# A selective scan on one core: GpSimd multiplies four state tiles by C in one instruction, and VectorE ends the softplus

## The reference

```python
xp = x @ W_xproj
dt, Bm, Cm = jnp.split(xp, [DT_RANK, DT_RANK + D_STATE], axis=-1)
dt = jax.nn.softplus(dt @ W_dt + b_dt)
A = -jnp.exp(A_log)
...
dA = jnp.exp(dt_t[:, :, None] * A)
dBu = (dt_t * u_t)[:, :, None] * B_t[:, None, :]
h = dA * h + dBu
y = jnp.einsum('bdn,bn->bd', h, C_t)
```

## Time and profile before

| | |
|---|---|
| median of 3 runs | 8623.25 us |
| the profiled execution: span | 8660.7 us |
| mean granted TensorE clock, as a share of 2.4 GHz | 0.819 |
| busy over the span: PE, DVE, ACT, POOL | 73%, 77%, 51%, 64% |
| first to last product by C (the middle stage) | 2617.2 to 8146.1 us |

### The profile page before, as it was taken

One profiled execution on the slowest core, in us unless ns is written; L12 is line 12 of the kernel. 1 busy time (PEld: TensorE's weight loads), 2 busy tenths in 40 slices (PEclk: granted clock), 3 DMA queues, 4 the chain that ended last, 5 costly groups with the idle time before them and its releaser, 6 DMA issues. The chain is left out here.

```text
span 8660.7 us, 103591 instructions
## 1 busy us (share of the span) xinstructions
PE 6299.7 (73%) x30668; PEld 2526.0 (29%) x30668; DVE 6682.6 (77%) x7810; ACT 4408.3 (51%) x5988; POOL 5534.1 (64%) x2731
## 2 busy tenths in 40 slices
PE   6888888888876667767767777767776666766455
PEld 3444444444431222222222222222222222222133
DVE  3555555555548999999999999999999999999634
ACT  1222222222226666666666666666666676766400
POOL 0000000000009999999999999999999999999600
PEclk8898888898887888888888888887888888778666
DMA  1111111111115556555555555555655555555553
GB/s 30 43 45 39 43 45 37 45 44 38 45 35 192 196 190 206 184 199 199 186 205 190 191 207 184 200 196 187 209 185 199 200 185 206 190 194 202 140 152 128
DMA packets 513971, 1253.45 MB, mean 145 GB/s; under 512 B 170085, under 2 KB 172297, under 8 KB 513673
## 3 DMA queue, kind: packets, MB, share of 16 engines
q1 hardware_dynamic: 513417, 1252.41, 43.5%
q0 software_dynamic: 512, 0.53, 0.0%
HBM read 943.30 MB, written 231.21 MB: 136 GB/s over the span
## 5 line engine op out<-in xcount | busy, mean ns | idle before, releaser
L1180 DVE TENSOR_TENSOR_SCAN b_h<-b_a,b_h 128x448 f32<-128x448 f32 x3584 | 3675.1, 1073 | 273.4 <-POOL b_h L1005 133.9
L1017 POOL TENSOR_TENSOR b_h<-b_h,b_ct 128x896 f32<-128x896 f32 x1792 | 3688.7, 2086 | 28.2 <-DVE b_h L1180 20.0
L1108 ACT ACTIVATE b_a<-b_dts,decay 128x441 f32<-128x441 f32 x3584 | 2228.2, 629 | 1579.4 <-DVE b_h L1180 1558.5
L1267 PE MATMUL b_b<-b_rows,spread_b 16*128 16x512 f32 (+1 forms) x1792 | 690.1, 778 | 1503.1 <-DVE b_h L1170 1502.1
L1028 POOL MEMSET b_seq<- 128x938 f32 x2 | 1.7, 880 | 2499.4 <-POOLq L792 2499.4
L1170 DVE TENSOR_TENSOR b_h<-b_dus,b_b 128x896 f32<-128x896 f32 x1344 | 1432.2, 1066 | 83.1 <-DMA b_dus<-d_dtu 77.7
L1275 PE MATMUL b_y<-b_h,fold 128*32 128x512 f32 (+1 forms) x7168 | 942.5, 652 | 7.8 <-POOL b_h L1017 7.8
L1005 POOL TENSOR_TENSOR b_h<-b_dus,b_bt 128x896 f32<-128x896 f32 x448 | 934.7, 2086 | 10.7 <-DMA b_dus<-d_dtu 10.7
L490 DVE TENSOR_TENSOR a_xg<-a_xd,a_pb 128x784 f32<-128x784 f32 x512 | 495.1, 967 | 512.0 <-PE a_pb L604 510.0
L1267 PEld LDWEIGHTS b_b<-b_rows,spread_b 16*128 16x128 f32 x1792 | 166.0, 226 | 1771.4 <-DVE b_h L1170 1769.8
L1236 PE MATMUL b_w<-b_seq,w_conv 128*128 128x384 f32 (+1 forms) x896 | 553.4, 781 | 12.6 <-DMA b_seq<-b_seq 12.6
(11 more groups left out here) (210 smaller groups left out, 8773.9 us busy)
## 6 DMA issues: line engine op xcount, KB each, us to landing
b_bt<-d_rows SPq DMA_DIRECT2D x448, 448.0 KB, 6.1
b_ct<-d_rows SPq DMA_DIRECT2D x448, 448.0 KB, 3.9
b_dts<-d_dt SPq DMA_DIRECT2D x448, 448.0 KB, 6.0
b_dus<-d_dtu SPq DMA_DIRECT2D x448, 448.0 KB, 6.1
a_xd<-a_xn SPq DMA_DIRECT2D x256, 196.0 KB, 3.4
d_dt<-b_dt SPq DMA_DIRECT2D x112, 448.0 KB, 2.6
d_dtu<-b_soft SPq DMA_DIRECT2D x112, 448.0 KB, 2.5
b_seq<-b_seq SPq DMA_DIRECT2D x112, 234.0 KB, 3.5
```

Source lines behind the costliest of these rows:

```text
L1017: nc.gpsimd.tensor_tensor(hh[t][:], hh[t][:], ct[t // 4 % 2][:], ALU.mult).then_inc(hc_done, 1)
L1108: a(steps(bank(aa, k)), steps(half(dts[t % 4], k)), ACT.Exp, scale=decay[:, t % 4, t // 4:t // 4 + 1]).then_inc(a_done, 1)
L1180: v.tensor_tensor_scan(half(hh[t], k), bank(aa, k), half(hh[t], k), 0.0, ALU.mult, ALU.add).then_inc(h_done, 1)
L1267: last = mm(bb[:, lo:hi], spread_b[q, row, :], rows[i][q, lo:hi], start=True, stop=True)
```

## The change

The 16 tiles `h[t]` become slices of one tile `h_all`. GpSimd multiplies a whole row (128 x 3584) in one instruction at t == 3, 7, 11, 15, C being read four times over. Softplus is written as max(v, ln(1 + exp(min(v, 20)))): with CAP = 20, ScalarE takes relu(CAP - v) out of PSUM, then Exp of CAP minus that, then Ln; VectorE takes the maximum of that and v, straight from PSUM (`step`), at t == 7. GpSimd keeps the product with u alone, behind t == 7. ScalarE's last four moves out of `b_w` come one tile later.

```diff
-                hh = ring("h", HH)
+                h_all = sb("h", [P, HH, TB])
+                hh = [h_all[:, t, :] for t in range(HH)]
...
                         def store_dt(par, o):
-                            sp.wait_ge(dt_ready, o)
+                            sp.wait_ge(moved, o)
...
-                        def products(j, o):
-                            pool.wait_ge(l_ready, o)
-                            nc.gpsimd.tensor_tensor(dtb[:], dtb[:], soft[:], ALU.add).then_inc(dt_ready, 1)
-                            pool.wait_ge(dt_ready, o)
+                        def step_input(j, c):
+                            pool.wait_ge(moved, c + 2)
                             nc.gpsimd.tensor_tensor(soft[:], dtb[:], u[j][:], ALU.mult).then_inc(dtu_ready, 1)
...
-                                pool.wait_ge(h_done, half_no(i, t, 1, it))
-                                nc.gpsimd.tensor_tensor(hh[t][:], hh[t][:], ct[t // 4 % 2][:], ALU.mult).then_inc(hc_done, 1)
-                                if t == 6 and more:
-                                    products(1 - i, unit_no(i, it) + 1)
+                                if t % 4 == 3:
+                                    pool.wait_ge(h_done, half_no(i, t, 1, it))
+                                    row = h_all[:, t - 3:t + 1, :]
+                                    nc.gpsimd.tensor_tensor(row, row, ct[t // 4 % 2][:].unsqueeze(1).broadcast_to([P, 4, TB]),
+                                                            ALU.mult).then_inc(hc_done, 4)
+                                if t == 7 and more:
+                                    step_input(1 - i, spot(i, "pre", it, kind))
...
                                 if t == 10 and i == 0 and kind != LAST:
-                                    sequences(spot(0, "z", it, kind), it + 1, tile_no(0, 10, it))
+                                    sequences(spot(0, "z", it, kind), it + 1, tile_no(0, 7, it))
...
                         def softplus_start(c):
                             act.wait_ge(made, c + 2)
-                            a(soft[:], ww[:, 0:TB], ACT.Abs, bias=dt_bias[:]).then_inc(abs_ready, 1)
-                            a(dtb[:], ww[:, 0:TB], ACT.Relu, bias=dt_bias[:]).then_inc(moved, 1)
+                            a(soft[:], ww[:, 0:TB], ACT.Relu, bias=dt_cap[:], scale=-1.0).then_inc(cap_ready, 1)
                         def softplus_end(o):
-                            act.wait_ge(abs_ready, o)
-                            a(soft[:], soft[:], ACT.Exp, scale=-1.0).then_inc(e_ready, 1)
+                            act.wait_ge(cap_ready, o)
+                            a(soft[:], soft[:], ACT.Exp, bias=cap_col[:], scale=-1.0).then_inc(e_ready, 1)
...
-                                if t == 8 and more:
+                                if t == 9 and more:
...
-                                if t == 10 and more:
+                                if t == 11 and more:
...
-                                if t == 12 and finals:
+                                if t == 13 and finals:
...
-                                if t == 14 and finals:
+                                if t == 15 and finals:
...
+                        def step(c, o):
+                            dve.wait_ge(l_ready, o)
+                            dve.wait_ge(made, c + 2)
+                            v.scalar_tensor_tensor(dtb[:], ww[:, 0:TB], dt_bias[:, 0:1], soft[:], ALU.add, ALU.max).then_inc(moved, 1)
...
+                                if t == 7 and not (kind == LAST and i == 1):
+                                    dve.wait_ge(dt_stored[i], 16 * it + 16 * i)
+                                    step(spot(i, "pre", it, kind), unit_no(i, it) + 1)
```

More of the change, by code:

```diff
@@ L44 @@
 RC = 8
+CAP = 20.0
 SMALL = 21
@@ L115, in program @@
         dt_bias = sbuf("dt_bias", [P, 1])
+        dt_cap = sbuf("dt_cap", [P, 1])
+        cap_col = sbuf("cap_col", [P, 1])
         decay = sbuf("decay", [P, 4, 4])
@@ L258, in _ @@
                     v.memset(one_col[:], 1.0).then_inc(zeroed, 1)
-                    dve.wait_ge(zeroed, 10)
+                    v.memset(cap_col[:], CAP).then_inc(zeroed, 1)
+                    dve.wait_ge(zeroed, 11)
                     dve.wait_ge(masks, 17)
@@ L291, in _ @@
                     link(v.tensor_copy(w_dt_full[:], pd[:, 0:DI]))
+                    link(v.tensor_scalar(dt_cap[:], dt_bias[:], -1.0, CAP, ALU.mult, ALU.add))
                     link(v.tensor_scalar(decay[:], decay[:], -1.0, -1e-12, ALU.mult, ALU.min))
@@ L785, in phase_b @@
                 sq_ready, rstd_ready, xn_ready, seq_ready = (sem(n) for n in ("sq", "rstd", "xn", "seq"))
-                abs_ready, e_ready, l_ready, dt_ready, dtu_ready = (sem(n) for n in ("abs", "e", "l", "dt", "dtu"))
+                cap_ready, e_ready, l_ready, dtu_ready = (sem(n) for n in ("cap", "e", "l", "dtu"))
                 skip_ready, yz_ready, gate_ready = (sem(n) for n in ("skip", "yz", "gate"))
@@ L900, in unit @@
                             if more:
-                                store_dt(par, o)
+                                store_dt(par, spot(i, "pre", it, kind) + 2)
                                 sp.wait_ge(moved, spot(i, "xp", it, kind) + 2)
@@ L939, in _ @@
                         shift_seq(1)
-                        store_dt(0, 2)
+                        store_dt(0, START.index("pre") + 2)
                         sp.wait_ge(moved, START.index("xp") + 2)
@@ L1004, in inputs @@
                             pool.wait_ge(folded, row_no(i, m, it) - 4)
-                            nc.gpsimd.tensor_tensor(hh[4 * m][:], dus[0][:], bt[m % 2][:], ALU.mult).then_inc(pb_done, 1)
+                            nc.gpsimd.tensor_tensor(hh[4 * m], dus[0][:], bt[m % 2][:], ALU.mult).then_inc(pb_done, 1)
                         def unit(i, it, kind):
@@ L1031, in _ @@
                         sequences(None, 1, None)
-                        products(0, 2)
+                        step_input(0, START.index("pre"))
                         inputs(0, 0, 1)
@@ L1120, in unit @@
                                 if t == 5 and more:
-                                    act.wait_ge(dt_stored[i], 16 * it + 16 * i)
                                     act.wait_ge(dtu_stored[i], 16 * it + 16 * i)
@@ L1169, in inputs @@
                                 dve.wait_ge(folded, row_no(i, t // 4, it) - 4)
-                            v.tensor_tensor(hh[t][:], dus[t % 4][:], bb[:, 0:TB], ALU.mult).then_inc(b_done, 1)
+                            v.tensor_tensor(hh[t], dus[t % 4][:], bb[:, 0:TB], ALU.mult).then_inc(b_done, 1)
                         def scan(t, i, it):
@@ L1213, in unit @@
                                     residual(spot(0, "out", it, kind), it - 1)
+                                if t == 7 and not (kind == LAST and i == 1):
+                                    dve.wait_ge(dt_stored[i], 16 * it + 16 * i)
+                                    step(spot(i, "pre", it, kind), unit_no(i, it) + 1)
                         v.memset(aa[:], 0.0).then_inc(aa_zero, 1)
+                        step(START.index("pre"), 2)
                         turns(unit)(dve)
```

## The result

The changed kernel takes 8847.76 us (median of 4 runs, 8829.70 to 8861.43) against 8624.98 us before: ratio 1.025, 95% interval 1.0228 to 1.0272. One of the four executions of the kernel before took 12958.84 us, and the ratio leaves it out. The changed kernel is slower by 2.5%, beyond the range on record (8495 to 8735). The profiled execution spans 8827.9 us.

What follows compares the result with a forecast made beforehand. GpSimd was taken as full and binding, 98.8 us a turn; the new circle summed 8.1 + 2.1 + 2.7 + 10.4 + 26.1 = 49.4 us a unit, 98.8 a turn, so no change: 8622 us, range 8495 to 8735.

Steps and rivals of the forecast that it cites:

- the circle: Row 1 on GpSimd, product with u, store, six loads, input 1, scan of tile 7: 49.4 us a unit.
- VectorE's floor: VectorE's own turn, with no wait for GpSimd or DMA: 96.1 us.
- GpSimd's saving: On GpSimd, row product 8.05 us and softplus add gone: turn 93.2 us, 5.6 less than now.
- VectorE's instruction: New VectorE instruction per unit at tile 7: 1.0 us, less 0.9 us of ScalarE wait, net 0.12 us a unit.
- The circle, first terms: From the end of the scan of tile 7: row 1 8.1 us, product with u 2.1, store and release 2.7.
- Six loads, 10.4 us: SyncE's loads dus 0 to dus 1 on the circle: 10.4 us, from 11.1 before less 0.7 for ct 3.
- The share of 1.00: DMA engines' share where these six loads run; taken to speak for the upper end between about 7.5 and 11.1 us.
- I cancel the two: Earlier sequences frees SyncE for dts 2 to dus 3, perhaps 0.3 us a unit; offset by queueing behind later loads.
- Rival 2: SyncE's queue between store of dt x u and dus 1: loads later still, 8701 to 8745 us; chance 0.13.
- Tied circles: Forecast case: both circles tied within 0.9 us a turn, no change, 8622 us, own range 8565 to 8680; chance 0.50.
- Rivals 3 and 4: TensorE's conv at the low clock each time, 8770, chance 0.05; GpSimd's row not cheaper, 8655 to 8728, chance 0.07.
- Rival 1: VectorE's own work sets the pace, dus 1 earlier or row shorter: 8473 us, partly reached 8475 to 8560; chance 0.25.

Runs made afterwards that it cites:

- row product alone, SyncE's order: Kernel before with the row product, SyncE storing dt x u ahead of rows and loading dus 0, bt 0, bt 1 ahead of ct 3: 8657.55 us, ratio 1.0022.
- dt x u first, SyncE's order: Changed kernel, product with u ahead of row 1, its store ahead of rows, dus 0, bt 0, bt 1 ahead of ct 3: 8566.2 us, ratio 0.9904.
- softplus part alone: Changed kernel with the product per tile put back and sequences waiting for tile 10 as before: 8552.63 us, ratio 0.9913.
- softplus part alone, SyncE's order: Changed kernel, product per tile, store of dt x u ahead of rows, dus 0, bt 0, bt 1 ahead of ct 3: 8606.62 us, ratio 0.9952.
- dt x u first: Changed kernel with one statement moved, the product with u ahead of row 1's product on GpSimd: 8622.63 us, ratio 0.9988.
- row product alone: Kernel before with GpSimd's row product, softplus as before, sequences waiting for tile 7: 8858.3 us, ratio 1.0246.
- changed, dus 1 ahead: Changed kernel with the load of dus 1 moved from sixth to second on SyncE's queue: 8809.12 us, ratio 1.0196.
- tiles, dt x u late: Changed kernel with product per tile, product with u behind tile 10's product, ct 3 loaded ahead of the store of dt x u: 9204.11 us, ratio 1.0652.

## Why the prediction was wrong

Two things are set side by side for every kernel. The first is how far behind the end of the scan of tile 7 dus 0 is issued, as a mean over the 92 to 103 units of each trace whose scan ends between 3000 and 8000 us. The second is VectorE's wait for dus in the stretch from 4400 to 5400.

| kernel | dus 0 issued, us behind | wait for dus, us a turn | ratio |
|---|---|---|---|
| row product alone, SyncE's order | 4.8 | 0.8 | 1.002 |
| dt x u first, SyncE's order | 5.0 | 0.6 | 0.990 |
| softplus part alone | 8.4 | 0.7 | 0.991 |
| softplus part alone, SyncE's order | 8.7 | 1.1 | 0.995 |
| dt x u first | 9.4 | 1.1 | 0.999 |
| before | 10.1 | 0.7 | 1 |
| row product alone | 12.3 | 5.1 | 1.025 |
| changed | 12.7 | 5.0 | 1.025 |
| changed, dus 1 ahead | 12.8 | 3.6 | 1.020 |
| tiles, dt x u late | 15.6 | 10.1 | 1.065 |

Up to about 10 us the wait is near nothing. From 12.7 to 15.6 each microsecond adds 0.9 us of wait to a unit. So the circle named under "what becomes late" is the cause, shown from both sides: with whole rows and no late dt x u the loss is gone, and with a late dt x u and no whole rows it is there. Below about 10 us it no longer decides, and the ratio follows other bounds: GpSimd's own work, its wait for ct 3, or VectorE's floor.

In the changed kernel VectorE waited for dus 1 at input 1 in all 98 of those units; before, in 20 of 101. So the circle closes in each, and its terms can be set against the forecast, from one scan of tile 7 to the next:

| term, us a unit | forecast | mean of 98 units |
|---|---|---|
| row 1 on GpSimd | 8.1 | 7.95 |
| the product with u | 2.1 | 2.03 |
| its store, to the issue of dus 0 | 2.7 | 2.70 |
| dus 0 issued to dus 1 landed | 10.4 | 11.42 |
| landing to the start of input 1 | 0 | 0.20 |
| input 1 to the end of the scan of tile 7 | 26.1 | 26.71 |
| sum | 49.4 | 51.01 |

Step by step:

- *GpSimd's saving*: right. A row takes 7.79 us against 8.05. My estimate of 7.9 by the Trainium skill, "GPSIMD Engine Reference", section 3.1, was the nearer; GpSimd's work in the stage is 91.1 us a turn (893.34 / 9.81).
- *VectorE's instruction*: nearly right. It takes 1.04 us from start to start, and the wait for ScalarE at tile 7 is gone; VectorE's work rose by 2.6 us a turn, not 2.0.
- *The circle, first terms*: right, 12.7 us to the issue of dus 0 where 12.9 was forecast. By luck the 0.2 us too much here cancels the 0.2 us from landing to input 1 that the sum had left out.
- *Six loads, 10.4 us*: here it failed. They took 11.4 us (11.9 in a unit i = 0, 10.9 in a unit i = 1). I took 0.7 us off the 11.1 seen before because ct 3 no longer sits right in front, and nothing had shown that this would help: the mean before is 11.3. Before, two issues were held back by tiles 12 and 13; now all come together. But in the units shown bt 0 to dus 1 land about 1.1 us apart in both kernels, so the earlier issues only wait longer: dus 1 lands 8.1 us behind its issue where it was 5.0. That is +2.0 us a turn.
- *The share of 1.00* that I took for the upper end belongs to 5036 to 5042, behind the six loads of a unit. Over the six of the earlier trace rows it was 0.82, and over those of the changed kernel it is 0.93 (first row before, second row changed; the number before the last):

```profile
5071.00:5083.00 12.00, 8.11 (x33) 2.73 (x34) 12.00 (x13) 7.62 (x12) 12.00 (x7) 0.80 0.82 288
5035.00:5047.00 12.00, 8.55 (x32) 2.82 (x31) 9.46 (x11) 6.74 (x10) 11.13 (x4) 0.64 0.93 325
```

- *"I cancel the two"*: here too it failed. dus 2 and dus 3 queue behind dus 1, with dts 2, ct 0 and dts 3 between. In the other unit of the turn inputs 2 and 3 waited a further 0.76 and 0.32 us (means 0.86 and 0.33). That is +1.2 us a turn. Both together are the 3.2 us by which the turn grew. On the forecast's 8622 us they make 8801, already outside the range; the rest up to 8848 is for the most part the scatter of the two profiled executions about their medians.
- *Rival 2* was the right story, with a chance of 0.13. It priced the loads at 11.1 to 11.5 us, which takes in the measured 11.4, and still had 8745 at its worst: it had no term for inputs 2 and 3, and the scatter between executions comes on top. The circle could gain only down to VectorE's floor, while every late term counts in full. Tied circles should have been weighed towards slower.
- *Rivals 3 and 4*: the wait ahead of `gated` did not grow (3.1 against 3.2 us a turn), conv took 5.1 us on average (570.3 / 112, before 4.9) and not 6.27, and the row was cheaper. Rival 1's floor of VectorE's own work is real, near 97 us a turn where 96.1 was forecast, and both kernels that reach it are faster than before.

Left open: that the transfers and not the issues set the time of the six loads is read from the times of their landings; no run separates it. Nor is it tried whether VectorE's waits for the fold and for ScalarE (2.3 and 1.5 us a turn at that floor) can be had as well.

## What to carry to other kernels

When instructions of a full engine are joined into a larger one, look at what stood between them. Here a small product that feeds a store and a reload was worth more than the time that the joining saved. Put the instruction with the longest way ahead of the long one, if its input is there; dt was ready 2.1 us before the row product began, about the length of the product with u, and the engine stood idle. A queue's order is part of the same step: a load that waits for the long instruction should not stand in front of the urgent ones. The same order cost 0.4% where the product was made tile by tile and needed that load early. And before calling two circles tied, count all transfers of the bunch at their spacing under load, and the inputs behind the first one that waits.

## What was not expected of the hardware

A GpSimd product of 3584 columns takes 7.79 us against 4 x 2.085 = 8.34, so joining four saves 0.55 us of busy time, or 0.18 for each instruction saved: nearly twice the 0.10 us that the memsets gave. From start to start the saving is smaller, some 0.4 us: six products in a row took 12.29 us, 2.05 each, and a row 7.76. Reading C four times over cost nothing that shows, though no row with four different tiles of C was run. Loads of 448 KB that are issued 0.6 us apart land about 1.1 us apart (bt 0 at 5042.1 to dus 1 at 5046.6, four steps).
